# The mean weight of layer 1's experts is put onto their results, and attentions 2 and 3 gather, normalise and write x in other slots

## The reference

```python
x = layernorm(x + attn(x));  x = layernorm(x + ffn(x))     # four times

# layer 1's attention: 16 heads of 8 features, weights from distances
d2 = maximum(q2[..., :, None] + k2[..., None, :] - 2 * qk, 1e-12)
out = softmax(-sqrt(d2)) @ v

# layer 1's feed-forward: 8 experts, each token goes to its two best
for e in range(8):
    mask = (topk_i == e).any(-1)
    mean_w = w_tok.sum() / maximum(mask.sum(), 1)      # one number for each expert
    eo = (silu(x @ gate_w[e].T) * (x @ up_w[e].T)) @ down_w[e].T
    out += mask * eo * mean_w

# layer 2's attention: grouped projections, 16 heads of 8, softmax(q k) v
# layer 3's attention: the same with dense projections, biases and a causal mask
```

## Time and profile before

| | us |
|---|---|
| median of 3 runs (lowest, highest) | 2982.04 (2979.73, 2988.38) |
| the profiled execution, its own time | 2990.81 |
| its span, first to last instruction | 2989.0 |
| TensorE, VectorE, ScalarE, GpSimd busy | 2366.8, 1513.0, 1441.0, 1281.6 |
| mean granted TensorE clock | 0.883 |

### The profile page before, as it was taken

The page is one execution under the profiler, slowest core; times in us unless marked ns, Lnnn a source line. Parts: engine busy times, 40 slices in busy tenths (PEclk is TensorE's granted clock), DMA queues, the critical chain, the costliest instruction groups (busy, mean ns, idle before and its releaser), DMA issues. The chain is left out here.

```text
span 2989.0 us, 52579 instructions
## 1 busy us (share of the span) xinstructions
PE 2366.8 (79%) x17978; PEld 1651.6 (55%) x17978; DVE 1513.0 (51%) x4235; ACT 1441.0 (48%) x3560; POOL 1281.6 (43%) x1908
## 2 busy tenths in 40 slices
PE   6999999993758999860898598896996999735860
PEld 4666666662745666540898244453553777524750
DVE  3555555553117999970233565673004666420653
ACT  4666666661427999950122154564221566511421
POOL 2444444444138777417432544431003444152255
PEclk9999999996867999985899687898997999967975
DMA  3000000002113222121111322220002322020222
GB/s 134 1 1 1 1 1 1 1 1 81 66 58 94 70 71 72 42 82 54 47 51 44 100 83 76 76 69 8 0 0 74 103 89 88 14 65 29 79 63 61
DMA packets 100387, 153.42 MB, mean 51 GB/s; under 512 B 16850, under 2 KB 69988, under 8 KB 93092
## 3 DMA queue, kind: packets, MB, share of 16 engines
q1 hardware_dynamic: 88356, 128.32, 13.8%
q0 software_dynamic: 11776, 21.81, 2.6%
HBM read 99.85 MB, written 48.24 MB: 50 GB/s over the span
## 5 line engine op out<-in xcount | busy, mean ns | idle before, releaser
L956 DVE TENSOR_REDUCE A_nmax<-A_S 128x2 f32<-128x512 f32 (+1 forms) x512 | 308.2, 620 | 213.7 <-PE A_S L757 100.3
L181 POOL TENSOR_SCALAR A_prob<-A_prob,A_rinv 128x256 f32<-128x256 f32 x512 | 236.7, 481 | 369.5 <-DVE A_rinv L433 369.4
L902 ACT ACTIVATE A_PT<-A_E 128x512 f32<-128x512 f32 (+1 forms) x512 | 276.3, 546 | 203.3 <-PE A_E L774 86.0
L428 DVE TENSOR_REDUCE A_nmax<-A_S 128x2 f32<-128x512 f32 x256 | 164.9, 686 | 160.5 <-PE A_S L271 160.5
L371 ACT ACTIVATE A_prob<-A_S,A_nmax 128x256 f32<-128x256 f32 x512 | 235.3, 479 | 4.7 <-DVE A_nmax L428 4.7
L1793 POOL COPY L_wr<-L_w 128x1024 f32 (+1 forms) x144 | 104.4, 727 | 247.4 <-PE L_k L1863 123.8
L1786 POOL DMA_INDIRECT sent<-x_state,row x160 | 154.9, 968 | 118.8 <-DVEq L2042 71.0
L1551 DVE TENSOR_SCALAR_CACHE_REDUCE A_D<-A_S 128x256 f32<-128x256 f32 x512 | 193.8, 418 | 13.1 <-PE A_S L1334 8.2
L1347 PE MATMUL A_T<-ident_sb,A_D 128*128 128x128 f32 x1024 | 159.7, 279 | 27.9 <-DVE A_PT L1557 16.8
L1557 DVE COPY A_PT<-A_T 128x512 f32<-128x512 f32 x256 | 175.2, 687 | 10.7 <-PE A_T L1347 10.2
L1960 ACT ACTIVATE L_silus<-L_k 128x512 f32<-128x512 f32 x72 | 43.0, 597 | 260.8 <-PE L_k L1863 260.8
(11 more groups left out here) (376 smaller groups left out, 6022.3 us busy)
## 6 DMA issues: line engine op xcount, KB each, us to landing
A_QS<-stack_q SPq DMA_DIRECT2D x144, 192.0 KB
A_KS<-stack_k SPq DMA_DIRECT2D x144, 192.0 KB
L_xe<-sent SPq DMA_DIRECT2D x46, 256.0 KB
results<-L_ye SPq DMA_DIRECT2D x46, 256.0 KB, 2.0
stack_q<-A_parts SPq DMA_DIRECT2D x48, 192.0 KB, 2.0
stack_k<-A_parts SPq DMA_DIRECT2D x48, 192.0 KB, 2.1
L_w<-f_w SPq DMA_DIRECT2D x24, 256.0 KB, 10.4
sent<-A_zeros SPq DMA_DIRECT2D x9, 512.0 KB
```

Of the source, the lines that this page charges most:

```text
L181: nc.gpsimd.tensor_scalar(prob[:, n % NP, j, t, :], prob[:, n % NP, j, t, :], rinv[:, n % NP, j, t:t + 1], 1.0, ALU.mult, ALU.mult).then_i ...
L428: nc.vector.tensor_reduce(nmax[:, n % NP, j, :], psS[n % 2][j][:], AX.X, ALU.max, negate=True).then_inc(maxed, 1)
L902: nc.scalar.activation(PT[:, n % RING, :], psE[n % 2][:, 0:BLOCKS, :].rearrange("p a b -> p (a b)"), ACT.Exp, scale=scale).then_inc(expd, 1)
L956: nc.vector.tensor_reduce(nmax[:, b % 2, :, h], view, AX.X, ALU.max, negate=True).then_inc(maxed, 1)
```

## The change

The places of a batch's early steps in `attention_small` are changed (X_AT is -35, a number mod 16 is the place inside a period). The gathers go from X_AT - 19 to X_AT - 35, the same place, one batch further ahead. `root_last` goes from -5 to -15, join and statistics from -8 and -7 to -18 and -17 for attention 2 and from -15 and -10 to -21 and -17 for attention 3, `write_last` from three slots ahead of X_AT to eleven ahead. At the end of a batch `root_var` is one slot later, `write_x` stands ahead of a row maximum in place of behind the slot's work and one slot later, and the turning of x for the next layer (`F_AT`) is two slots later. In `attention_dist` `write_x` is on GpSimd, right behind `root_var`. In the experts of layer 1 the mean weights are looked up for each tile (`tile_mean`) and multiplied onto the results in `take_y`, and so `join_rows` in attention 2 only adds, with one operation over both tiles of a batch.

```diff
-    F_AT, LG_AT = Y_AT + 9, Y_AT + 12
+    F_AT, LG_AT = Y_AT + 11, Y_AT + 13
     SLOTS = NB * H
-    GET_AT, NORM_AT = X_AT - 19, X_AT - 5
-    JOIN_AT, STATS_AT = (X_AT - 8, X_AT - 7) if last["K"] else (X_AT - 15, X_AT - 10)
+    GET_AT, NORM_AT = X_AT - 35, X_AT - 15
+    JOIN_AT, STATS_AT = (X_AT - 18, X_AT - 17) if last["K"] else (X_AT - 21, X_AT - 17)
...
# attention_small, GpSimd's loop
+                    if (b := at(s, Y_AT + 4)) is not None:
+                        root_var(b)
                     if (b := at(s, H + 1)) is not None:
                         split_max(b)
...
-                    if (b := at(s, Y_AT + 3)) is not None:
-                        root_var(b)
...
# attention_small, VectorE
                     for k in range(K):
-                        after(dve, joined_x, JOINED * b + TB * k if k else 0)
-                        for tile in range(TB):
-                            nc.vector.scalar_tensor_tensor(out=ly(b)[:, tile, :], in0=lrows[:, b % 2, tile, k, :],
-                                                           scalar=last["weight"][:, k, TB * b + tile:TB * b + tile + 1],
-                                                           in1=ly(b)[:, tile, :] if k else x_state[:, TB * b + tile, :],
-                                                           op0=ALU.mult, op1=ALU.add).then_inc(joined_x, 1)
+                        after(dve, joined_x, K * b + k if k else 0)
+                        nc.vector.tensor_tensor(ly(b), lrows[:, b % 2, :, k, :], ly(b) if k else x_state[:, TB * b:TB * (b + 1), :], ALU.add).then_inc(joined_x, 1)
...
-                    if (b := at(s, NORM_AT + 2)) is not None:
+                    if (b := at(s, NORM_AT + 4)) is not None:
                         write_last(b)
+                    if (b := at(s, Y_AT + 9)) is not None:
+                        write_x(b)
                     if (n := head(s)) is not None:
                         row_max(n)
...
-                    if (b := at(s, Y_AT + 8)) is not None:
-                        write_x(b)
...
# attention_dist: taken out of VectorE's loop (slot Y_AT + 7), put into GpSimd's
                     if (b := at(s, Y_AT + 3)) is not None:
                         root_var(b)
+                        write_x(b)
...
# routed_layer, mean_weights
-                    for k, sel in enumerate((sel1, sel2)):
-                        link(nc.vector.tensor_tensor(d[:], sel[:], over_t(mean), ALU.mult))
-                        link(nc.vector.tensor_reduce(weight[:, k, :], d[:], AX.X, ALU.add))
+                    link(nc.vector.tensor_tensor(past[:], numbers[:, 0:E].unsqueeze(1).to_broadcast([P, Q, E]),
+                                                 tile_of[:].unsqueeze(2).to_broadcast([P, Q, E]), ALU.is_equal))
+                    link(nc.vector.tensor_tensor(past[:], past[:], mean[:].unsqueeze(1).to_broadcast([P, Q, E]), ALU.mult))
+                    nc.vector.tensor_reduce(tile_mean[:], past[:], AX.X, ALU.add).then_inc(meant, 1)
...
# routed_layer, take_y
+                    elif mean2:
+                        dve.wait_ge(meant, 1)
+                        i = nc.vector.tensor_tensor(ye[:, q % 2, :, :], by_tile(psY[q % 2]),
+                                                    tile_mean[:, QUAD * q:QUAD * (q + 1)].unsqueeze(2).to_broadcast([P, QUAD, P]), ALU.mult)
                     else:
                         i = nc.vector.tensor_copy(ye[:, q % 2, :, :], by_tile(psY[q % 2]))
```

More of the change, by code:

```diff
@@ L568, in attention_small @@
         NMSTEPS = 4
-        JOINED = TB * K if K else 1
+        JOINED = max(K, 1)
         loads = [(wqk[:], w["wqk"]), (wv[:], w["wv"]), (wo[:], w["wo"]), (bo[:], w["bo"].partition_broadcast(P))]
@@ L983, in norm_stats, with join_rows, write_last @@
                         nc.vector.bn_aggr(mv[:, t, :], stats[:, t, :]).then_inc(y_steps, 1)
+                def join_rows(b):
+                    dve.wait_ge(fetched[b % 2], 16 * TB * K * (b // 2 + 1))
+                    after(dve, x_ready, TB * (b - 1))
+                    for k in range(K):
+                        after(dve, joined_x, K * b + k if k else 0)
+                        nc.vector.tensor_tensor(ly(b), lrows[:, b % 2, :, k, :], ly(b) if k else x_state[:, TB * b:TB * (b + 1), :], ALU.add).then_inc(joined_x, 1)
+                def write_last(b):
+                    dve.wait_ge(l_rooted, 2 * b + 2)
+                    for tile in range(TB):
+                        nc.vector.tensor_scalar(x_state[:, TB * b + tile, :], ly(b)[:, tile, :], lmv[:, b % 2, tile, 0:1], lrstd[:, b % 2, tile:tile + 1],
+                                                ALU.subtract, ALU.mult).then_inc(x_ready, 1)
                 def write_x(b):
@@ L989, in write_x @@
                                                 ALU.subtract, ALU.mult).then_inc(x_done, 1)
-                def join_rows(b):
-                    dve.wait_ge(fetched[b % 2], 16 * TB * K * (b // 2 + 1))
-                    after(dve, x_ready, TB * (b - 1))
-                    for k in range(K):
-                        after(dve, joined_x, JOINED * b + TB * k if k else 0)
-                        for tile in range(TB):
-                            nc.vector.scalar_tensor_tensor(out=ly(b)[:, tile, :], in0=lrows[:, b % 2, tile, k, :],
-                                                           scalar=last["weight"][:, k, TB * b + tile:TB * b + tile + 1],
-                                                           in1=ly(b)[:, tile, :] if k else x_state[:, TB * b + tile, :],
-                                                           op0=ALU.mult, op1=ALU.add).then_inc(joined_x, 1)
-                def write_last(b):
-                    dve.wait_ge(l_rooted, 2 * b + 2)
-                    for tile in range(TB):
-                        nc.vector.tensor_scalar(x_state[:, TB * b + tile, :], ly(b)[:, tile, :], lmv[:, b % 2, tile, 0:1], lrstd[:, b % 2, tile:tile + 1],
-                                                ALU.subtract, ALU.mult).then_inc(x_ready, 1)
                 def stats_last(b):
@@ L1035, in _ @@
                         norm_stats(b)
-                    if (b := at(s, Y_AT + 8)) is not None:
-                        write_x(b)
-                    if onward["gate"] is not None and (b := at(s, LG_AT + 1)) is not None:
+                    if onward["gate"] is not None and (b := at(s, LG_AT)) is not None:
                         take_logits(b)
@@ L1232, in root_var, with write_x @@
                     nc.gpsimd.tensor_tensor(rstd[:], veps[:], mhalf[:], ALU.pow).then_inc(rooted_var, 1)
+                def write_x(b):
+                    pool.wait_ge(rooted_var, 2 * b + 2)
+                    for t in range(TB):
+                        nc.gpsimd.tensor_scalar(x_state[:, TB * b + t, :], y[:, t, :], mv[:, t, 0:1], rstd[:, t:t + 1],
+                                                ALU.subtract, ALU.mult).then_inc(x_done, 1)
                 def get_last(b, i):
@@ L1580, in norm_stats @@
                         nc.vector.bn_aggr(mv[:, t, :], stats[:, t, :]).then_inc(y_steps, 1)
-                def write_x(b):
-                    dve.wait_ge(rooted_var, 2 * b + 2)
-                    for t in range(TB):
-                        nc.vector.tensor_scalar(x_state[:, TB * b + t, :], y[:, t, :], mv[:, t, 0:1], rstd[:, t:t + 1],
-                                                ALU.subtract, ALU.mult).then_inc(x_done, 1)
                 def stats_last(b):
@@ L1615, in _ @@
                         norm_stats(b)
-                    if (b := at(s, Y_AT + 7)) is not None:
-                        write_x(b)
 def routed_layer(nc, layer, x_state, consts, w, dram, held, XT):
@@ L1700, in routed_layer @@
             wsum, mean, silus = sb("wsum", [P, E]), sb("mean", [P, E]), sb("silus", [P, 2, F])
+            tile_mean, meant = sb("tile_mean", [P, Q]), sem("meant")
         if cap2:
```

## The result

The changed kernel takes 3025.40 us in the median of 4 runs (3017.74 to 3039.66), the kernel before beside it 2983.08 (2979.73 to 2988.38). The ratio is 1.0146, 95% interval [1.010, 1.0192]: 1.5% slower, outside the range and on the other side. The profiled execution of after took 3031.96 us, its span is 3030.2 us and its mean clock 0.865 against 0.883. A later set of runs made the loss larger: there before took 2884.65 us and the same changed kernel 2967.61, ratio 1.0278 [1.0257, 1.0298].

What follows compares the result with a forecast made beforehand. Attention 1 was taken as bound by VectorE and ScalarE, attention 2 by stalls with half clock behind them. Terms -1 + 0 - 1 - 8.7 - 1.5 = -12.2 us on 2990.8 gave 2978.6, median 2970 (2961 to 2977); range 2930 to 2994.

Steps and rivals of the forecast that it cites:

- attention 2 under way: Attention 2's batches: gathers one batch further ahead, everything before the stall unchanged, one stalled group less, -8.7 us.
- The mechanism was among the rivals: Attention 2: normalising and join without a row maximum between, 1.7 us, make TensorE wait; +23 us, 3005; chance 0.18.
- A sign that failed: Attention 2: the prediction is wrong if TensorE's waits for row maxima double, from 20.8 us in 27 waits.
- One group less under the stall, -8.7 us: Attention 2: the last gathers go out one period sooner, so one group less meets the VectorE stall, -8.7 us.
- the 70 us that I hung on the gathers: Attention 2: eight gather groups lie in 1770 to 1960, so some 70 us hang on what the change moves.
- 3.8 + 5.15 met the 8.7: Attention 2: a 3.8 us wait plus 5.15 us from half clock account for 8.7 us more per gathering batch.
- Attention 1, -1 us: Attention 1: x's write on GpSimd frees VectorE, -2.0 under way, +1.0 at the end; sum -1, bounds -3 and +4.
- Layer 1's weights, 0: Feed-forward 1 and attention 2's join: mean weight on the results and shorter join change nothing; feed-forward bounds -1 and +2.
- Start of attention 2, -1 us: Attention 2's start: third x no longer late, split 0 2.5 us later, stack next late; -1, bounds -5 and +2.5.
- attention 3, -1.5 us: Attention 3: root 1 ahead of split 0 on GpSimd lets split 1 start sooner; -1.5, bounds 0 and -5.

Runs made afterwards that it cites:

- write_slot4: Changed kernel with VectorE's write of the incoming x two slots later in attentions 2 and 3: 2961.91 us, ratio 0.9884; in a later set 2874.38 us, 0.9963.
- gathers_later: Changed kernel with the write of the incoming x at its old place, and gathers in attentions 2 and 3 five slots later: 2893.59 us, ratio 1.0031.
- slot4_dist_undone: write_slot4 with attention 1's write of x back on VectorE: 2872.85 us, ratio 0.9959.
- before_again: The kernel before itself, unchanged, run again for its trace in a later set: 2885.87 us, ratio 1.0003.
- slot4_mean_undone: write_slot4 with layer 1's weights as before (weight for each choice, copies, weighted join of four operations): 2881.82 us, ratio 0.9993.
- write_slot10_again: Changed kernel with the write of the incoming x at its old place, twelve slots behind the root, taken again: 2875.89 us, ratio 0.9967.

## Why the prediction was wrong

- **The step that failed** is the one on attention 2 under way, "Everything in front of the stall looks as before". The stretch of the new order that stood ahead of the prediction begins with the write on line 995, and I did not ask what is in front of it. The offsets say it: `norm_stats` at Y_AT + 2 = 65 ends slot 1 of a period, and the write at NORM_AT + 4 = -46 opens slot 2. I summed the pieces between row maxima at one place only (normalising and join, 1.7 us) and not here, where the durations of the trace of before add up to 0.42 + 0.49 + 0.30 + 0.60 = 1.8 us, and 2.36 came out because the write was stretched beside GpSimd's split to 1.38. It was a term of its own, at zero in my sum, and without the stall it measured +5.5 us in most periods of attention 2 and +1.4 to +4.3 in attention 3.
- **The mechanism was among the rivals**, with the right price for the clock (5.15 us) and the wrong place. It had 0.18, and 3005 us. At the place that I named, a piece of 1.77 us costs nothing in write_slot4 and lost the clock in two batches of gathers_later; with 2.14 two batches of nine lose it, with 2.36 in attention 2 all thirteen of the two traces do, and with 2.44 in attention 3 two or three of nine. So the length of the piece alone doesn't decide, and a slot of 1.0 us was too low as the bound; what TensorE has in hand beside the scores (turned scores, the product with v) may be why, which no run isolates.
- **A sign that failed:** I was to be wrong if TensorE's waits for row maxima doubled. They did not: 20.8 us in 27 waits before, 23.0 in 16 after, and without the stall 23.5 in 50 and 28.5 in 28, all from 1760 to 1955. The sum of the waits hides that a few have become long enough to take the clock down.
- **One group less under the stall, -8.7 us**: not shown. The stall was absent in four later sets, with the kernel before at 2883 to 2886 us, so the 70 us that I hung on the gathers were a condition of those runs. They were also too many: a period under the gathers takes 18.5 us without any stall, for the 16.0 behind them, so a stall was 24.7 - 18.5 = 6.2 us and not 8.7, and that 3.8 + 5.15 met the 8.7 was chance. Where no stall is, gathering sooner is worth 0.2% [0.1, 0.3] in the kernel before. In the set with stalls write_slot4 gained 1.2% [0.8, 1.5]; whether by fewer stalls is likely from its periods, but no run isolates it.
- **Attention 1, -1 us**: the mechanism is as said, the size is below what the runs can tell. GpSimd's write took 1.58 us at the end, as worked out; VectorE is 0.8 us a batch freer (235.26 us busy for 243.51) and ScalarE is not (243.66 for 242.99); slot4_dist_undone shows no difference. VectorE's writes had been stretched beside GpSimd's work, to 1930 ns where 335 is the shortest. The Trainium skill, SBUF — State Buffer, section Who interferes with whom, says that a VectorE instruction in a mode that takes both of its ports and a GpSimd instruction block each other for the whole instruction, and that tensor_scalar, which this write is, can be in such a mode. The stretch agrees with it; which mode the write is in no run shows. It decided nothing there.
- **Layer 1's weights, 0**: mis-sized. This part wins 0.3%, by the shorter join in attention 2: about half by keeping a piece below 2.14 us, and 3 us by VectorE's time in a stage whose VectorE I had called free at 127.8 of 195.0 us. That share was taken under the stall; without it VectorE is busy 163.5 of 195.0.
- **Start of attention 2, -1 us, and attention 3, -1.5 us**: both 0 up to the first row maximum. From the stage's start to the first row maximum are 43.6 us for 43.3, and 35.0 for 34.9. The third x comes at 1676 to 1678 and not near 1668: its root on GpSimd stands behind split 0 and the gathers of batch 3, and VectorE waits 6.40 us for it. The stack is what is late, as said. In attention 3 VectorE's waits for the root fell from 18.7 to 3.4 us, as forecast, and split 1 began 6.2 us behind split 0 for 10.1. What that is worth under way is hidden by the loss in the changed kernel; the whole of attention 3 took 347.5 us in write_slot4_again for 349.0 in before_again, in one trace each.

## What to carry to other kernels

When steps are moved between slots, add up for each engine the time between two of the instructions that feed the next engine (here the row maxima), not the engine's load: VectorE was busy for well under nine tenths and still cost 1.5 to 2.8%, by one piece of 2.4 us a period. Price the piece with the stretched duration of its instructions, and price a pause of TensorE with the half clock behind it. A stall that a trace shows may be a condition of those runs: two sets had this one and the next four did not. So take the kernel before again, with its trace, in each set that is built to explain a stall.

## What the runs showed of the hardware

- A pause of TensorE of 1.2 us in slot4_mean_undone was followed by 10.1 us at 0.50, and one of 1.7 us in the changed kernel by 23 us at 0.50, a stretch that takes in the next group of gathers. In attention 3 most pauses of about 1.4 us left the clock at 1.00, a few did not, and of nine equal pauses of 1.2 us in slot4_mean_undone seven did.
- VectorE's write of the incoming x (128x128, two a batch) took 340 ns in the median in write_slot10_again and up to 1201 ns in write_slot4_again, beside GpSimd's split. Beside GpSimd's gathers, in before, it was not stretched: 340 ns in the median, 526 at most.
- The same program took 2983 to 2992 us in two sets of runs and 2883 to 2886 in four. In the longer ones TensorE stood still while GpSimd's indirect transfers were under way. In attention 2 that is the stall behind each group of four gathers. It is plainer in the experts of layer 3, where GpSimd issues 64 indirect sends in a row. Windows of before, and of before_again at the same work:

```profile
2642.00:2682.00 40.00, 12.52 (x58) 7.31 (x56) 0.69 (x1) 2.75 (x4) 30.26 (x33) 0.71 0.16 53
```

```profile
2583.00:2623.00 40.00, 40.00 (x221) 28.63 (x220) 4.15 (x6) 15.67 (x23) 30.33 (x32) 0.99 0.16 53
```

  GpSimd and the bytes moved are the same; TensorE is busy 12.52 us in the one and 40.00 in the other. VectorE's waits on line 2103 in this stage, in before with TensorE's own beside it, then in before_again:

```profile
DVE L_acc L2103 <- remote: 68.2, 1, 68.2
PEld L_k L1839 <- issue: 66.7, 16, 57.4
```

```profile
DVE L_acc L2103 <- PE L_k L1839: 47.9, 8, 6.3
```

  In before the profile doesn't know who releases VectorE ("remote"), and TensorE's own 57.4 us in one piece are time in which it waited for nothing that the profile shows ("issue"). So that the transfers hold TensorE is read from the two lying side by side and not shown, and why it is so in some sets and not in others stays open: the kernels built for it ran when it was absent. The profile that the prediction was read from was of the longer kind.
